# Attention output divided by its sums with features on partitions, two images at a time, with sums moved by DMA and new order tables

## The reference

```python
h = concat([patch_tokens(x), txt], axis=1)      # 64 x (9 + 1 + 77) x 256
y = layernorm(h)
q, k, v = split(y @ w_qkv.T)                    # 16 heads of 16
q, k = rope(layer_norm(q)), rope(layer_norm(k))
attn = softmax(q * 16**-0.5 @ k.T)              # per image and head, 87 x 87
h = h + (attn @ v) @ w_proj.T + b_proj
y = layernorm(h)
w = softmax(y @ gate_w.T); keep the two largest of 8
h = h + y @ W_lin.T + b_lin + sum_e w[e] * (y @ left[e]) @ right[e]
```

## Time and profile before

| what | value |
|---|---|
| median of 3 runs | 741.35 us |
| span of the profiled execution, first to last instruction | 734.0 us |
| own device time of the profiled execution | not recorded; the median stands 7.35 us over the span |
| busy: TensorE, VectorE, GpSimd, ScalarE | 673.9, 531.2, 491.0, 432.0 us (92, 72, 67, 59%) |
| chain that ended last | PE 71%, DVE 12%, issue 4%, ACT 4%, SyncE's queue 3%, POOL 3%, DMA 2% |
| DMA | 58.73 MB, 69528 packets, of these 30607 under 512 B |
| mean granted TensorE clock | 0.967 of full speed |

### The profile page before, as it was taken

How to read it: one execution, slowest core, us unless ns; L and a number is a source line. 1 busy time by engine, 2 the same in 40 slices (tenths; PEclk the granted TensorE clock), 3 DMA queues, 4 the chain that set the end, 5 groups by cost and what they waited for, 6 DMA issues and landing times.

```text
span 734.0 us, 24407 instructions
## 1 busy us (share of the span) xinstructions
PE 673.9 (92%) x9431; PEld 564.8 (77%) x9431; DVE 531.2 (72%) x1192; ACT 432.0 (59%) x1115; POOL 491.0 (67%) x564
## 2 busy tenths in 40 slices
PE   5998998999985799999999999999999999999873
PEld 3987887888853577888888888888888888887652
DVE  2468687887978646788878878878878887866642
ACT  4553452635442346677777676677776777776541
POOL 3667563764648428787877877876976977975442
PEclk9999999999996969999999999999999999999996
DMA  8963472231011223223232332332332332122001
GB/s 222 237 163 116 129 224 47 54 83 44 22 24 40 59 54 79 63 70 82 67 78 73 75 83 73 79 82 72 78 83 68 79 86 67 42 54 62 26 25 34
DMA packets 69528, 58.73 MB, mean 80 GB/s; under 512 B 30607, under 2 KB 68646, under 8 KB 69286
## 3 DMA queue, kind: packets, MB, share of 16 engines
q1 hardware_dynamic: 69414, 57.18, 30.9%
HBM read 33.69 MB, written 11.40 MB: 61 GB/s over the span
## 4 chain that ended last, share of the span: by engine, by line
PE 71%; DVE 12%; issue 4%; ACT 4%; SPq 3%; POOL 3%; DMA 2%; POOLq 0%; DVEq 0%; ACTq 0%
PE p_a L1355 13%; PE p_c L1355 10%; PE p_conv L758 8%; PE p_kv L758 7%; PE p_o L1427 6%; PE p_s L1415 5%; PE p_mm L758 4%; PE p_s L1397 4%; PE p_n L1435 3%; PE p_c L1474 3%; PE p_a L1381 3%; PE p_s L1411 2%; DVE t L1282 2%; DMA kr<-qkT 2%; DVE kv L656 1%
## 5 line engine op out<-in xcount | busy, mean ns | idle before, releaser
L1291 DVE TENSOR_REDUCE mx<-p_s 87x16 bf16<-87x1392 f32 x64 | 102.5, 1602 | 44.6 <-PE p_s L1397 44.4
L1214 ACT ACTIVATE prT<-p_s 87x1392 f32<-87x1392 f32 x64 | 85.2, 1331 | 29.3 <-PE p_s L1415 27.8
L1121 POOL TENSOR_TENSOR t<-t,ss_rs 116x512 f32<-116x512 f32 x48 | 50.9, 1060 | 58.9 <-ACT ss_rs L1190 57.8
L426 POOL TENSOR_TENSOR xs_lo<-xcols,xs_hi 120x585 fp32r<-120x585 f32 (+1 forms) x45 | 60.4, 1348 | 43.7 <-ACT xs_hi L483 43.7
L1415 PE MATMUL p_s<-qr,kr 32*87 32x87 f32 x2048 | 68.8, 257 | 0.0
L1115 POOL TENSOR_TENSOR t<-t 116x512 f32<-116x512 f32 x48 | 62.4, 1299 | 5.6 <-DVE t L1282 5.6
L1135 POOL TENSOR_TENSOR yT_lo<-y_raw,yT_hi 128x232 fp32r<-128x232 f32 x48 | 32.5, 678 | 47.1 <-issue 31.4
L1124 POOL TENSOR_TENSOR t<-t,tabs 116x512 f32<-116x512 f32 x48 | 61.2, 1276 | 2.7
L1415 PEld LDWEIGHTS p_s<-qr,kr 32*87 32x87 f32 x2048 | 60.3, 154 | 0.0
L1411 PE MATMUL p_s<-mxT,pick_row 32*87 32x87 bf16 x1024 | 55.7, 208 | 1.9 <-ACT mxT L1208 1.9
L1427 PE MATMUL p_o<-prT,vp 87*32 87x87 f32 x2048 | 55.1, 248 | 0.1
(11 more groups left out here) (287 smaller groups left out, 2077.8 us busy)
## 6 DMA issues: line engine op xcount, KB each, us to landing
xcols<-in_x_cols SPq DMA_DIRECT2D x12, 822.7 KB, 8.1
h<-h_tokens SPq DMA_DIRECT2D x16, 348.0 KB
out<-out_sb SPq DMA_DIRECT2D x48, 116.0 KB
...
x<-in_txt_cols SPq DMA_DIRECT2D x32, 154.0 KB, 4.1
qr<-qkT SPq DMA_DIRECT2D x64, 58.0 KB, 2.0
kr<-qkT SPq DMA_DIRECT2D x64, 58.0 KB, 2.0
...
```

Of the source, the lines that this page charges most:

```text
L426: nc.gpsimd.tensor_tensor(xs.lo[:, n % XS_SLOTS, :, 0:M].bitcast(F32R), raw, xs.hi[:, n % XS_SLOTS, :, 0:M], ALU.subtract).then_inc(S['xs_ ...
L1214: nc.scalar.activation(prT[:, k % 2], p_s[0:SEQ, :, 0:QUADS * SEQ], ACT.Exp, scale=HD ** -0.5).then_inc(S['s_exp'], 1)
L1291: nc.vector.reduce_max(mx[:, k % 2, :, 0:QUADS], p_s[0:SEQ, :, 0:QUADS * SP].rearrange("p j (a k) -> p j a k", k=SP)[:, :, :, 0:SEQ], AX_X ...
```

## The change

- oN and oB go. Instead of tokens on partitions, the division is made with features on partitions. oT of two images (k = 0, 1 or 2, 3) is written side by side; SyncE's new step `part` moves values and sums of this pair to two tiles of equal layout with four DMAs; `rd` (ACT) takes 1/sum as exp(−ln(sum)) in place, `norm` (DVE) multiplies, `on` (ACT) and `on_lo` (POOL) make high and low part. Each runs twice a group in place of four times. The rows of w_proj are reordered on the host to match.
- The ones stand in vt beside the values and are moved with them: transfers are twice as wide and are cut at multiples of 16 rows, 12 a group in place of 6. place has 4 transfers a group in place of 16, for the same bytes.
- lora becomes one single-pass product per tile: tw holds the inputs three times, twT transposes each tile, `tw_lo` (DVE) turns one copy into the low part, and `right_3` holds high, high and low part of `right`.
- p_n is free and serves as second bank beside p_c (`TILE_BANKS`).
- All order tables are new, of windows and groups, with starts written out (`WINDOW_AT`, `GROUP_AT`).

```diff
+                if name == 'part':
+                    n2 = 2 * g + k + 1
+                    sp.wait_ge(S['o_out'], 2 * n2)
+                    wait(sp, S['o_norm'], n2 - 2)
+                    for side in range(2):
+                        for n in range(2):
+                            sp.dma_start(parts[side:P:2, k, n], oT[n:P:2, k, side:4:2]).then_inc(o_in[k], 16)
...
+                    for side in range(2):
+                        sp.dma_start(strips[0:P:2, half, side, :, c0:c1], qkT[64 * side:64 * (side + 1), half, :, c0:c1]).then_inc(k_in[half][k], 16)
...
+                    for b, t, n0, n1 in PIECES_OF_ROWS[k]:
+                        sp.dma_start(vp[n0 - SEQ * b:n1 - SEQ * b, half, b].rearrange("p d n h -> p (d n h)"),
+                                     vt[n0 - TP * t:n1 - TP * t, half, t].rearrange("p d n h -> p (d n h)")).then_inc(v_in[k], 16)
...
                 if name == 'oT':
                     wait(act, S['pv'], n4)
-                    wait(act, S['oN'], n4 - 2)
-                    nc.scalar.copy(oT[:, k % 2], p_o[:, 0:4 * SEQ].rearrange("p (c q) -> p c q", c=4)).then_inc(S['o_out'], 1)
-                if name == 'oB':
...
+                    wait(act, o_in[k // 2], 64 * g)
+                    nc.scalar.copy(oT[:, k // 2, :, k % 2], p_o[:, 0:4 * SEQ].rearrange("p (c q) -> p c q", c=4)).then_inc(S['o_out'], 1)
+                if name == 'rd':
+                    act.wait_ge(o_in[k], 64 * (g + 1))
+                    wait(act, S['o_norm'], 2 * (g - 1) + k + 1)
+                    link(nc.scalar.activation(parts[:, k, 1], parts[:, k, 1], ACT.Ln))
+                    nc.scalar.activation(parts[:, k, 1], parts[:, k, 1], ACT.Exp, scale=-1.0).then_inc(S['rd_ok'], 1)
+                if name == 'on':
+                    wait(act, S['o_norm'], 2 * g + k + 1)
...
+                    nc.scalar.copy(onT.hi[:, half, :, 2 * SEQ * k:2 * SEQ * (k + 1)].bitcast(F32R), on[:, k].rearrange("p c b q -> p c (b q)")
+                                   ).then_inc(S['on_high'], 1)
...
                 if name == 'norm':
-                    link(nc.vector.reciprocal(rd[:], o3[:, :, HD]))
...
+                    nc.vector.tensor_tensor(on[:, k], parts[:, k, 0], parts[:, k, 1], ALU.mult).then_inc(S['o_norm'], 1)
...
+                if name == 'tw_lo':
...
+                    nc.vector.tensor_tensor(twT[lows].bitcast(F32R), product('gate', g, k)[lows, 0:GT].rearrange("p (t n) -> p t n", t=TILES),
+                                            twT[lows], ALU.subtract).then_inc(S['tw_low'], 1)
...
-                if name == 'oN':
...
-                if name == 'oB':
...
+                    pe.wait_ge(S['on_low'], 2 * g + min(k, 1) + 1)
...
-                        mm_ = nc.tensor.matmul(product('lora', g, k)[0:TP, n * C:(n + 1) * C], twT[:], right[:, tile], start=True, stop=True)
+                        mm_ = nc.tensor.matmul(product('lora', g, k)[0:TP, n * C:(n + 1) * C], twT[:, tile].bitcast(F32R),
+                                               right_3[:].bitcast(F32R), start=True, stop=True)
```

More of the change, by code:

```diff
@@ L247, in wait @@
         engine.wait_ge(semaphore, n)
[L250 to L259, removed]
@@ L906, in patch_tokens @@
     return sync, gpsimd, scalar, vector, tensor, S
-GROUP_ACT = table("""xhi.0.-132 sq.0.-26 rstd_a.0.14 sq.1.37 rstd_r.0.56 v.0.102 v.1.120 qkT.0.139 rstd_r.1.152 sq.2.165 qkT.1.203
-                v.2.221 rstd_r.2.238 qkT.2.284 mT.0.320 exp.0.338 mT.1.383 exp.1.401 oT.0.435 mT.2.448 exp.2.466
-                oT.1.510 mT.3.525 oT.2.536 exp.3.542 oB.0.575 oB.1.633 oT.3.647 oB.2.662 oB.3.734 yT.0.762
-                yT.1.778 rstd_c.0.875 ffn.0.881 ffn.1.904 yT.2.916 ffn.2.944 gate.0.1004 twT.0.1086""")
@@ L913 @@
-GROUP_DVE = table("""stats.0.-202 stats.1.-176 stats.2.-169 eps.0.-130 rotate.0.-17 ss.0.43 rotate.1.58 ss.1.114 rotate.2.173
-                ss.2.201 max.0.292 max.1.361 max.2.427 max.3.499 norm.0.522 norm.1.561 norm.2.603 norm.3.688
-                h2.0.733 h2.1.749 stats_c.0.791 stats_c.1.805 h2.2.861 stats_c.2.866 logits.0.950 rank.0.996
-                weigh.0.1038 out.0.1104 out.1.1109 out.2.1248""")
-GROUP_PE = table("""qk.0.-48 qk.1.19 v.0.84 qkT.0.131 qk.2.148 qkT.1.194 v.1.211 qkT.2.277 peak.0.281 mT.0.315 scores.0.325
-                peak.1.353 mT.1.378 scores.1.388 pv.0.412 peak.2.419 mT.2.444 scores.2.453 oN.0.475 peak.3.482
-                pv.1.497 mT.3.520 pv.2.522 scores.3.529 oN.1.548 oB.0.569 oN.2.587 oB.1.611 pv.3.622 oB.2.651
-                oN.3.674 oB.3.715 proj.0.722 proj.1.739 yT.0.756 yT.1.771 proj.2.838 ffn.0.869 ffn.1.890
-                yT.2.911 ffn.2.932 twT.0.1072 lora.0.1092 lora.1.1232""")
@@ L1082, in clear_strips @@
                 pool.wait_ge(W['conv'], CONVS)
-                for part in (qr, kr, mx):
+                for part in (strips, mx):
                     ready(nc.gpsimd.memset(part[:], 0.0))
@@ L1254, in step @@
                     wait(act, S['lora'], 2 * g)
-                    nc.scalar.copy(twT[0:TILES * LR], product('gate', g, k)[0:TILES * LR, 0:TP]).then_inc(S['twT_out'], 1)
+                    nc.scalar.copy(twT[0:3 * LR].bitcast(F32R), product('gate', g, k)[0:3 * LR, 0:GT].rearrange("p (t n) -> p t n", t=TILES)
+                                   ).then_inc(S['twT_out'], 1)
             return step
@@ L1303, in step @@
                     dve.wait_ge(S['hb_ok'], n3)
+                    if g == 0 and k == 0:
+                        for part in range(2):
+                            dve.wait_ge(W[f'st_rows{part}'], ROWS_OUT * len(range(part, STEPS, 2)))
                     nc.vector.tensor_tensor(h2[:, half, k], product('tile', g, k)[0:TP, 0:C], hb[:, k], ALU.add).then_inc(S['h2_ok'], 1)
```

243 lines of the change are left out of this document (124 added, 119 removed).

## The result

The changed kernel took 909.89 us (median of 4 runs, 907.86 to 914.63), the kernel before 741.23 us beside it (4 runs, 739.83 to 742.57): 1.229 times the time, 95% interval 1.223 to 1.234. The profiled span is 906.4 us against 734.0.

The account below looks back on a forecast made before the run. TensorE was full, with the score-bank ring close behind; in the new order ScalarE's steps before exp bound it. 31.7 ring + 2.0 place wait + 1.0 clock = 34.7 us a group against 28.2; 84 + 8 more gave 833 us, range 775 to 888.

Parts of the forecast that it names:

- low clock (860 and over): Rival: half of the TensorE-bound work at 1.2 GHz adds some 5 us a group, 885 us; chance 0.16.
- The ring: Per group, four images: peak to mT (B) 10.96 plus mT to next peak (A) 20.75, 31.7 us against 28.2.
- DMA on the ring: Peak.0 waits for place.0, queued on SyncE behind four part transfers: 2.0 us a group, bounds 0.8 to 3.0.
- The clock: TensorE spells at 1.2 GHz, costing only where TensorE is waited for: 1.0 us a group, bounds 0 and 15.
- TensorE's own work: Fewer transpositions and a one-pass LoRA product: −3.0 us a group, a gain only where TensorE is waited for.
- VectorE and GpSimd: Their changed steps in a group: cost 0, between −0.5 and +0.5 us, both idle over 8 us a period.
- Windows 0, tail 0: New window tables cost 0 for the stage (−5 to +10 us); last group's tail 0 (−3 to +5).
- Groups 0, 1 and 15: First two and last groups, with shorter ScalarE lists: +8 us together.
- Values hidden: The 12 values transfers, formerly 6, queue behind place.0 and are used later: hidden; otherwise 6 × 0.6 us on pv.
- ring alone: Rival: period 31.7 us without transfer wait or clock loss, 791 us (780 to 810); chance 0.19.
- shorter ring: Rival: ScalarE's steps overlap more or rd costs half, period 29.5 us, about 763 us (743 to 780); chance 0.15.
- faster: Rival: TensorE stays what is waited for and its 3.0 us a group are kept, 698 us; chance 0.07.

Follow-up runs that it names:

- e11: Changed kernel with place.0 ahead of part.0 on SyncE and unread matmuls ahead of the four peaks of a group: 815.7 us, ratio 1.093 to 1.105.
- e1: Changed kernel with SyncE's place.0 moved ahead of part.0 of the group before: 834.96 us, 1.131 times the kernel before.
- e4: Changed kernel with 30, 16, 24 and 6 unread matmuls ahead of the four peaks of a group: 863.01 us, ratio 1.159 to 1.180.
- e5: Changed code with the adapted group order tables of the kernel before and the new window tables: 741.2 us, ratio 0.998 to 1.007.
- e9: e5 with max.3 ahead of weigh and h2.1 in VectorE's order: 741.13 us, ratio 0.9961 to the kernel before.
- e6: e5 with the window tables of the kernel before as well: 740.12 us, ratio 0.998 to 1.006.
- e8: e5 with the values in 6 uncut transfers a group instead of 12: 752.17 us, against 741.2.
- e12: e9 with unread matmuls, 10 ahead of each of the last six pv, 16 ahead of each later TensorE step of the last group: 773.96 us.

## Why the prediction was too low

The direction and the places of the waits were right; the size was not: 909.9 where 833 stood, and 888 was the end of the range. The steps that failed are two terms of the sum for a group: the wait for the place transfer, put at 2.0 and measured at 3.6, and the clock, put at 1.0 where about 4.8 is left for it. The result fell into the case "low clock (860 and over)", which had a chance of 0.16.

- *The ring, 31.7.* Right. At full clock (e11) B was 10.91 for 10.96, and A of k=0 to 2 was 6.06, 5.75, 5.02 for 6.0, 6.0, 4.8. In the kernel after, A came to 6.66, 6.04, 4.99. For k=2 the sum is right by luck in part: it took ScalarE's 4.8 and did not count TensorE's own 4.9 in the same stretch. The two operations of rd occupy 0.92 (569.79 to 570.71) for 0.85.
- *DMA on the ring, 2.0 with bounds 0.8 and 3.0: mis-sized.* Between exp.3 and peak.0 stand 3.97 us, where e1 has 0.37: 3.6, above the upper bound. Where it came from, in means over groups 2 to 14: oT.1 ended 2.65 after peak.3, as good as the 2.55 of the prediction. The four part issues took 2.95 and not 2.44, since an issue took more than its price of 0.61 (the rows of 542 to 553 show 3.2 for four), and the second place issue started 6.6 after peak.3 and not 5.6. Its 232 KB took 4.0 us to land, where the 2.0 contain 3.3 (8.9 − 5.6): I had taken a value between 2.0 (58 KB) and 4.1 (154 KB), though the transfer is larger than either.
- *The clock, 1.0 with bounds 0 and 15: mis-sized.* What is left of the period is 40.1 − 31.7 − 3.6 = 4.8, and 3.7 of it is B (14.66 for 10.96). Idle matmuls alone gave back 2.7 (e4). e1, with a clock of 0.88, still has 3.6 over 31.7, so the shorter pause gave back 1.2. With both, and a clock of 1.00 (e11), B and A of k=0 to 2 are those of the prediction: the 4.8 is the clock to within a few tenths, and the two terms are not independent. That is inside the bounds, and the rival that priced it at 5 had it right. The earlier trace rows held the evidence: TensorE 72% busy and then 0.50. The Trainium skill, TensorE: Matmul & The Clock Gate (HAM oscillation), weighed against that as seen once only, was the better guide: with pauses of 1.7 us in the mean at 46 peaks and of 4.8 at 16, the page of the kernel after shows a clock between 0.7 and 0.9 in nearly every slice of the group stage.
- *TensorE's own work, −3.0, a gain only where it is waited for.* As said; the LoRA product fell from 27.9 us to 14.4, 0.84 a group for 0.95. Even in the old order no time came of it (e5), and 0.7 a group at most (e9).
- *VectorE and GpSimd, 0.* Right in the new order, where both have idle time. Not in the old one: weigh's third product made max.3 late there (e5).
- *Windows 0, tail 0.* Near enough: −5.5 before the first max, just past the bound of −5, and +0.2 behind the last. The −5.5 seem to belong to the order of the first groups and not to the window tables: with the old order of the groups the first max stands at 251.9 with the new window tables (e5) and at 247.7 with the old (e6). The whole times of e6 and e5 differ by 0.15%.
- *Groups 0, 1 and 15: +8.* Too small: they cost 16.0 + 6.7. The prediction gave them shorter lists and no price of their own for the two terms above.
- *Values hidden.* Right as to the ring; e8 shows that uncut they would not be.

In all: 13 × (40.1 − 34.7) = 70, +15 for the other groups, −5 up to the first max is 80 of the 80 us between the forecast span, 826, and 906.4. The 7.35 us from span to median was no constant either: the median after stands 3.5 over its span, and every execution whose core span is on record took 1.7 to 1.8 us more than that span, so the profiled execution of the kernel before, with its span of 734.0, took about 736 us and not the median. The 0.2% that was to tell a difference from nothing was too fine as well: beside the experiments the kernel before took 733 to 747 us. Of the rivals, ring alone, shorter ring, faster and no change are refuted for this order. Still open: which pauses cost how much of the 4.8 (e4 and e1 alone account for 3.9), and the clock in the tail of e9 and e12.
